# A sparse-graph layer and an eight-expert feed-forward layer in one kernel: the order of Pool's work round the last routing, and the gate's logits in one product with the turn

## The reference

```python
h  = item_feat @ W_item.T + b_item                    # 10000 x 128
x1 = x + relu(adj @ h + layernorm(x) @ W_user.T + b_user)

t      = layernorm(x1)
logits = t @ gate_w + gate_b                          # 8 experts
idx    = argmax(softmax(logits)); prb = its probability
pos    = place of the token among those of its expert, in token order
kept   = pos < 1563                                   # capacity
y      = relu(t @ w1[idx] + b1[idx]) @ w2[idx] + b2[idx]
out    = x1 + y * prb * kept                          # a token beyond capacity keeps x1
```

## Time and profile before

| | |
|---|---|
| three runs | 1380.58, 1382.54, 1383.38 us; median 1382.54 |
| the profiled execution | 1382.88 us, of which the span of its instructions is 1381.1 us |
| busy share of the span | PE 97%, DVE 85%, ACT 68%, Pool 42% |
| granted TensorE clock, mean | 0.984 |
| HBM | 428.11 MB read, 23.87 MB written, 327 GB/s over the span |

### The profile page before, as it was taken

The page is one execution under the profiler, slowest core; times in us unless marked ns, Lnnn a source line. Parts: engine busy times, 40 slices in busy tenths (PEclk is TensorE's granted clock), DMA queues, the critical chain, the costliest instruction groups (busy, mean ns, idle before and its releaser), DMA issues. The chain is left out here.

```text
span 1381.1 us, 19857 instructions
## 1 busy us (share of the span) xinstructions
PE 1339.5 (97%) x6152; PEld 1097.9 (79%) x6152; DVE 1169.4 (85%) x1781; ACT 945.8 (68%) x906; POOL 576.0 (42%) x335
## 2 busy tenths in 40 slices
PE   7999999999999999999999999999999999899993
PEld 6888888888888888888888888888888877677772
DVE  6999989899898898988989989889898894577774
ACT  5777767767667677676776767767767664677871
POOL 0001154262450633605426145162360563588887
PEclk9999999999999999999999999999999999899997
DMA  8999999999999999999999999999999985233220
GB/s 327 359 379 405 412 397 373 372 370 379 367 367 377 359 379 369 366 384 360 375 375 366 380 364 372 372 363 372 378 363 376 366 302 162 80 100 100 71 49 3
DMA packets 99950, 441.56 MB, mean 320 GB/s; under 512 B 29635, under 2 KB 37867, under 8 KB 99905
## 3 DMA queue, kind: packets, MB, share of 16 engines
q1 hardware_dynamic: 69017, 418.17, 80.3%
q0 software_dynamic: 24928, 12.59, 3.8%
q10 hardware_dynamic: 5960, 10.24, 2.3%
HBM read 428.11 MB, written 23.87 MB: 327 GB/s over the span
## 5 line engine op out<-in xcount | busy, mean ns | idle before, releaser
L694 DVE TENSOR_TENSOR a_lo<-raw,a_hi 128x2000 fp32r<-128x2000 f32 (+1 forms) x400 | 867.7, 2189 | 101.4 <-ACT a_hi L501 96.7
L501 ACT CAST a_hi<-raw 128x2000 fp32r<-128x2000 f32 (+1 forms) x400 | 724.8, 1826 | 287.1 <-PE bank L1109 189.5
L1107 PE MATMUL bank<-a_hi,h_hi 128*128 128x500 f32 x1560 | 622.7, 399 | 0.6 <-ACT a_hi L501 0.6
L1109 PE MATMUL bank<-a_hi,h_lo 128*128 128x500 f32 x1560 | 607.5, 389 | 0.0
L1118 PE MATMUL bank<-a_lo,h_hi 128*128 128x500 f32 x1560 | 419.0, 389 | 0.0
L1107 PEld LDWEIGHTS bank<-a_hi,h_hi 128*128 128x128 f32 x1560 | 294.3, 189 | 63.2 <-issue 5.7
L1109 PEld LDWEIGHTS bank<-a_hi,h_lo 128*128 128x128 f32 x1560 | 294.9, 189 | 60.5 <-issue 4.4
L1118 PEld LDWEIGHTS bank<-a_lo,h_hi 128*128 128x128 f32 x1560 | 293.9, 188 | 59.6
L1003 POOL TENSOR_TENSOR late<-ve,neghalf 125x4 f32<-125x4 f32 x20 | 55.3, 2763 | 597.5 <-DVE ve L711 597.5
L1011 POOL DMA_INDIRECT records<-late,slot x80 | 170.3, 2129 | 22.8 <-issue 22.8
L1075 POOL DMA_INDIRECT out<-raw x104 | 144.4, 1388 | 43.9 <-issue 33.6
(11 more groups left out here) (128 smaller groups left out, 848.0 us busy)
## 6 DMA issues: line engine op xcount, KB each, us to landing
raw<-adj_m SPq DMA_DIRECT2D x380, 1000.0 KB, 6.5
raw<-adj_m SPq DMA_DIRECT2D x20, 500.0 KB
xT<-x_t ACTq DMA_DIRECT2D x20, 250.0 KB, 4.2
late<-items_t SPq DMA_DIRECT2D x19, 256.0 KB, 4.5
raw<-records SPq DMA_DIRECT2D x24, 191.8 KB
xb<-x ACTq DMA_DIRECT2D x20, 224.0 KB
raw<-w SPq DMA_DIRECT2D x8, 258.5 KB
raw<-w SPq DMA_DIRECT2D x8, 256.0 KB
```

Of the source, the lines that this page charges most:

```text
L501: last = nc.scalar.copy(a_hi[:, g % HI_RING, 0:m], raw[:, g % RAW, 0:m])
L694: last = v.tensor_tensor(a_lo[:, g % RAW, 0:m], raw[:, g % RAW, 0:m], a_hi[:, g % HI_RING, 0:m].bitcast(F32), ALU.subtract)
L1107: nc.tensor.matmul(acc[q][:, 0:BLOCK], h_hi[:, k * HID:(k + 1) * HID], a, start=(k == 0), stop=False)
L1109: last = nc.tensor.matmul(acc[q][:, 0:BLOCK], h_lo[:, k * HID:(k + 1) * HID], a, start=False, stop=False)
```

## The change

Six things change.

1. `logits` and `turn_x1` become one product: the constants' table puts `gate_w` right behind the identity, so four matmuls by 136 columns give the turned x1 and its logits. They go to two PSUM banks, two tiles each; ACT copies them with two instructions in place of one, and `choose` on DVE scales the logits with two in place of one.
2. In block 19 this product for block 18 stands at g = 3, where logits and turn stood at g = 2.
3. `find_order` on DVE stands at g = 8 of block 19, not 14.
4. Pool issues `pass_on` of block 17 ahead of the wait for the cleared slots, and `pass_on` of block 18 ahead of `x1_scale` of block 19.
5. Slots are cleared in 120 runs of 14 for each expert (1680 slots), not 124 of 13 (1612); `clear_edges` has 112 rows, not 104.
6. Units 0 and 1 are turned back, gated and put out inside the routing of block 19, not in steps 5 and 6.

```diff
-RUN = 13
-RUNS = SLOTS_E // RUN
+RUN = 14
+RUNS = 120
+SLOTS_E = RUNS * RUN
...
+        turn_w = cst[:, COLS["ident"][0]:COLS["gate_w"][1]]
...
-                nc.scalar.copy(rec[:, q, :, 0:HID],
-                               turned[0:TP, :].rearrange("p (j d) -> p j d", j=TILES)).then_inc(x1_ready, 1)
+                for half, turned in enumerate(ps_turn_last if is_last(n) else ps_turn):
+                    last = nc.scalar.copy(rec[:, q, 2 * half:2 * half + 2, 0:HID], turned[:, :, 0:HID])
+                last.then_inc(x1_ready, 1)
...
-                dve.wait_ge(logits_done, n + 1)
+                dve.wait_ge(x1_ready, n + 1)
...
-                        if g == 14:
+                        if g == 8:
                             find_order()
...
-                if has(at, LAG_OUT, 0):
+                if at == EARLY + LAG_IN:
+                    gate_and_add(0, 0)
+                if at == EARLY + LAG_MID:
+                    gate_and_add(0, 1)
+                if has(at, LAG_OUT):
                     gate_and_add(i, k - LAG_OUT)
...
                     clear_slots()
                     clear_edges()
+                    pool.wait_ge(slots_ready, b - 1)
+                    pass_on(q)
                     pool.wait_ge(edges_cleared, 16)
                     pool.wait_ge(runs_cleared, EXPERTS * 16)
                 if not fixed or b > 1:
                     scatter(b - 2, q)
+                if not fixed or 1 < b < BLOCKS - 1:
                     pass_on(q)
...
             scatter(BLOCKS - 2, 0)
+            pass_on(0)
             x1_scale(BLOCKS - 1, 1)
-            pass_on(0)
             scatter(BLOCKS - 1, 1)
...
-            def logits(n):
+            def turn_x1(n):
                 pe.wait_ge(x1T_ready, n + 1)
                 if not isinstance(n, int) or n > 0:
+                    pe.wait_ge(x1_ready, n)
                     pe.wait_ge(shifted, n)
-                to = ps_logit_last if is_last(n) else ps_logit
+                turned = ps_turn_last if is_last(n) else ps_turn
                 for j in range(TILES):
-                    last = nc.tensor.matmul(to[:, j, :], gnn[:, j * TP:(j + 1) * TP], const("gate_w"),
+                    last = nc.tensor.matmul(turned[j // 2][:, j % 2, :], gnn[:, j * TP:(j + 1) * TP], turn_w[:, :],
                                             start=True, stop=True)
...
-                    if g == (2 if is_last(b) else 5) and (not fixed or b > 0):
-                        logits(b - 1)
+                    if g == (3 if is_last(b) else 5) and (not fixed or b > 0):
                         turn_x1(b - 1)
```

More of the change, by code:

```diff
@@ L47 @@
 UNIT = max(UNIT_TILES) * SLOT_P
-SLOTS_E = UNIT_AT[-1]
-assert SLOTS_E >= CAP and UNIT <= 512
+RUN = 14
+RUNS = 120
+SLOTS_E = RUNS * RUN
+assert SLOTS_E >= UNIT_AT[-1] >= CAP and UNIT <= 512
 SLOTS = EXPERTS * SLOTS_E
 UNITS = EXPERTS * UNITS_E
-RUN = 13
-RUNS = SLOTS_E // RUN
 EDGE = EXPERTS * RUN
-assert SLOTS_E % RUN == 0 and max(RUNS, EDGE) <= TP
+assert max(RUNS, EDGE) <= TP
 BODY = 2 * UNITS_E
@@ L74 @@
 _at = 0
-for _name, _n in (("ident", 128), ("tri", TP), ("rev", TILES * EXPERTS), ("tok", 2 * TILES),
-                  ("w_user", HID), ("gate_w", EXPERTS), ("gate_b", TILES * EXPERTS),
+for _name, _n in (("ident", HID), ("gate_w", EXPERTS), ("tri", TP), ("rev", TILES * EXPERTS), ("tok", 2 * TILES),
+                  ("w_user", HID), ("gate_b", TILES * EXPERTS),
                   ("run_at", 1), ("run_no", EXPERTS), ("edge_of", EXPERTS),
@@ L202, in build @@
         acc = bank[0:2]
-        ps_gnn, ps_x, _, ps_h0, ps_h1 = bank[2:7]
-        ps_logit, ps_logit_last = (t[0:TP, 2 * EXPERTS:(2 + TILES) * EXPERTS].rearrange("p (j e) -> p j e", j=TILES)
-                                   for t in (bank[4], bank[7]))
+        _, ps_x, _, ps_h0, ps_h1 = bank[2:7]
+        TURN = HID + EXPERTS
+        ps_turn, ps_turn_last = ([t[0:TP, a:a + 2 * TURN].rearrange("p (j c) -> p j c", j=2) for t, a in pair]
+                                 for pair in (((bank[2], 0), (bank[4], 0)),
+                                              ((bank[6], 0), (bank[7], 2 * EXPERTS))))
         ps_count = bank[7][0:TP, 0:EXPERTS]
@@ L657, in _ @@
             v = nc.vector
-            chain = Chain(dve, dve_chain, 22)
+            chain = Chain(dve, dve_chain, 23)
             x_chain = Chain(dve, x_chain_done, 2)
@@ L746, in choose @@
                 chain.round(n)
-                dve.wait_ge(logits_done, n + 1)
+                dve.wait_ge(x1_ready, n + 1)
                 dve.wait_ge(rstd_ready, n + 1)
-                raw_logit = ps_logit_last if is_last(n) else ps_logit
-                chain.link(v.tensor_tensor(lg[:, :, :], raw_logit, rec[:, q, :, C_RSTD:C_RSTD + 1].broadcast_to(
-                    [TP, TILES, EXPERTS]), ALU.mult))
+                for half, turned in enumerate(ps_turn_last if is_last(n) else ps_turn):
+                    pair = slice(2 * half, 2 * half + 2)
+                    chain.link(v.tensor_tensor(lg[:, pair, :], turned[:, :, HID:TURN],
+                                               rec[:, q, pair, C_RSTD:C_RSTD + 1].broadcast_to([TP, 2, EXPERTS]),
+                                               ALU.mult))
                 chain.link(v.tensor_tensor(lg[:, :, :], lg[:, :, :], gate_b, ALU.add))
@@ L1269, in _ @@
             turn_slots(0, 2)
+            turn_y(0, 0)
             second(0, 1, range(2, FC))
@@ L1276, in step @@
                     mid(i, k - LAG_MID)
-                if has(at, LAG_OUT, 0):
+                if at == EARLY + LAG_MID:
+                    turn_y(0, 1)
+                if has(at, LAG_OUT):
                     turn_y(i, k - LAG_OUT)
```

12 lines of the change are left out of this document (removed).

## The result

| | before | changed | changed, second comparison |
|---|---|---|---|
| median, us | 1382.96 | 1368.19 | 1370.27 (before: 1382.91) |
| runs | 4 | 4 (1366.81 to 1370.40) | 6 (1367.78 to 1371.33) |
| ratio, 95% interval | | 0.9898 (0.9879 to 0.9917) | 0.9908 (0.9890 to 0.9925) |
| profiled execution: time, span | 1382.88, 1381.1 | 1370.40, 1368.5 | span 1368.0 |

The changed kernel is faster, by 14.8 us in the first comparison and 12.6 in the second; the forecast was 13. The profiled execution, against whose time the sum was made, became 12.5 us shorter. What follows reads the changed kernel's trace against the rows of before.

What follows compares the result with a forecast made beforehand. PE bounds the blocks and units, and a chain through Pool's clearing DMAs the stretch between. Terms -5.5 + 0.2 - 8.4 + 0.6 = -13.1 us from 1382.88 give 1369.8, forecast 1370, range 1365 to 1378.

Steps and rivals of the forecast that it cites:

- The product: Logits and turn on PE: the joint product saves 0.31 us a block in 18 blocks, -5.5 us.
- The slower joint product: Rival: weight loads not hidden, the joint product takes 1.70 us and costs 8.8 us, total 1387 to 1391; chance 0.04.
- ACT's and DVE's additional instructions: About 0.2 us each, costing nothing beside PE in the blocks; DVE's stands on the chain behind block 19, +0.2 us.
- Block 19: g = 2 to 9: PE's lead is lost in a new wait of 4 to 5 us and slow clock; worth 0.
- The first weights: Order known some 18 us earlier: SP's loads start at 1146.7, about 5.7 us earlier, removing PE's 3.3 us wait for tokens.
- The clears: Landing of Pool's slot-clearing DMAs moves from 1158.93 to 1150.5, -8.4 us.
- both causes act at once: Less adjacency ahead of the clears and more evenly loaded DMA engines together: landing at 1150.5.
- the even end of 1148.5: Landing of the clears at about 1148.5 if all DMA engines were evenly loaded.
- x1_scale follows the landing one to one: Pool's twelve DMAs stay in between, so `x1_scale` of block 19 gains what the landing gains, 8.6 us at most.
- Units 0 and 1: Turned and gated inside block 19's routing: +0.6 us, between -1 and +2, with PE waiting up to 2 us.
- the clears land where they did: Rival: the landing doesn't improve, the tail gains between -1 and 4, total 1374 to 1378; chance 0.27.
- HBM bounds the blocks: Rival: HBM loads bound the blocks, the shorter product gives nothing, only the tail is left, 1375.5; chance 0.08.

Runs made afterwards that it cites:

- e1: The kernel before with only the joint product of logits and turn (point 1), still at g = 2 in block 19: 1375.01 us, ratio 0.9944.
- e7: The changed kernel with `find_order` at g = 11 of block 19 instead of g = 8: 1370.22 us, ratio 0.9925.
- e2: The changed kernel with the old clearing geometry, 124 runs of 13 slots and edges of 104 rows: 1375.27 us, ratio 0.9951.
- e9: The changed kernel with 116 clearing runs of 14 slots instead of 120, edges unchanged: 1376.53 us, ratio 0.9952.
- e5: The kernel before with only the joint product and 120 clearing runs of 14 slots, all else in the old order: 1371.70 us, ratio 0.9936.
- e11: The changed kernel run again, unaltered: 1370.27 us, ratio to the kernel before 0.9908.
- e6: The changed kernel with point 4 undone, Pool's `pass_on` of blocks 17 and 18 in their old places: 1369.05 us, ratio 0.9914.
- e3: The changed kernel with point 6 undone, units 0 and 1 turned and put out behind the routing: 1366.52 us, ratio 0.9887.
- e4: The changed kernel with `x1_scale` of block 19 ahead of Pool's `pass_on` of block 18: 1365.74 us, ratio 0.9881.
- e8: The changed kernel with the edits of e3 and e4 together: 1363.63 us, ratio to the kernel before 0.9878.
- e12: e8 run again, on the same chip as e11: 1363.78 us, ratio to the kernel before 0.9868.
- e10: e8 with `find_order` back at g = 14 of block 19: 1366.38 us, ratio to the kernel before 0.9884.

## Why the prediction was right

The mechanisms of the sum stood, and its total, but two of its terms were mis-sized, in opposite directions.

- **The product, forecast -5.5: measured -7.9** in the changed kernel's trace, 6.8 to 8.3 in all (e1: -8.2 for the whole kernel). The step that failed is the interpolation from the 372-column records. The eight records take 0.84/8 = 0.105 us each, which is what the transposes' took with 128 columns and about what the logits' took with 8 (0.099): in these rows the columns of a record, from 8 to 136, hardly matter. So the joint product costs what the eight logits' records had cost, and the transposes' 0.43 us is nearly all saved. The prediction had this case as its bound of 0.4 us a block and took the interpolated 0.31. The slower joint product, the rival that ended on the other side, is excluded.
- **ACT's and DVE's additional instructions: nothing in the blocks**, as said. The 0.2 us behind block 19 weren't measured by themselves.
- **Block 19, forecast 0: right.** The new wait is 3.45 us, forecast 4 to 5, ended by `pick`. PE is ready for the first tokens 7.8 us earlier, the blocks' part. e7 adds why its size hardly matters here: what PE gains in block 19 it gives back at the next count.
- **The first weights.** Forecast at 1146.7 - 5.5 = 1141.2, measured 1139.38, of which 2.4 us is the product's other size. PE's wait for the tokens is gone, as said. But the early order isn't enough for it: e2 and e9 know the order as early, and load the first weights at 1143.23 and 1142.17, after which PE waits 1.48 and 1.42 us. The forecast had no part of the geometry in this term.
- **The clears, forecast -8.4: measured -4.4.** The step that failed is "both causes act at once". The closed gap in the adjacency's loads gave nothing by itself: e2 has it, and its clears land at 1151.53, where before's less the 7.9 of the blocks would be at 1151.03. The 120 rows, and so, by the inference above, the even load of the engines, gave it (4.9 us in e2, 4.1 in e9; in the old order 2.5, e5 against e1), and less than the even end of 1148.5 that was reckoned: with the 7.9 us of the blocks added back the landing was at 1154.5, where the sum had 1150.5. The prediction also had the even load alone, 3.4 us and a landing at 1155.5, and should have taken that.
- **x1_scale follows the landing one to one: right** in before and in every run that kept `x1_scale` behind the twelve DMAs (18.6 to 19.3 us). Forecast at 1163.5, measured 1165.25.
- **Units 0 and 1, forecast +0.6 (-1 to +2): measured +1.8 us**, and 3.6 where the clock falls. The waits for the low parts were named, 2 us at most; the low clock behind them wasn't priced.
- **The sum**: -7.9 and -4.4 are -12.3, and the count of block 19 is 12.2 us earlier. Behind it, where point 6 costs, the profiled execution lost nothing against before. Before had its own slow clock there (0.50 from 1180 to 1190), and e1, with 0.56 from 1170 to 1180, takes 199.85 us behind its count, as before does; that the two make up for each other isn't shown further. Two errors of 2.4 and 4.0 us with opposite signs and two small ones made 13.1 where 12.5 was measured. That the total came out so near is luck: the forecast was nearer than its steps.
- **The rival "the clears land where they did"** is out; "HBM bounds the blocks" is out by e1: the product alone brought 8.2 us at the end, and PE had no gap in the blocks at a DMA share of 0.99.

## What to carry to other kernels

- Where a wait is for the landing of many small indirect DMAs, try their number of rows before their bytes or their order: here 120 rows in place of 116 or 124 were worth 4 to 5 us of landing in the new order and 2.5 in the old, while the reordering around them was worth nothing without it.
- Reordering one queue pays only if the instruction that others wait for is the one moved forward. Pool's new order exchanged four DMAs for four and gained nothing; with `x1_scale` moved to the front of them it gained 2.4 to 4.5 us.
- Work put into a gap of one engine must fit on all engines it uses. Units 0 and 1 fitted PE's gap, and filled DVE's, which the next unit needed.

## What the runs showed that was not expected

- **The number of rows also sets the time of issue.** Pool takes 0.99 us for a clearing DMA of 120 rows (the shortest of eight), 1.26 with 116 and 1.31 with 124 (e9, e2). And Pool's own queue has fewer packets with 120 rows than with 116 or 124 (24928 in e2): its entry in the profile's third part is, for e9,

```profile
q0 software_dynamic: 24672, 12.64, 4.0%
```

  and for the changed kernel, with 32 rows more,

```profile
q0 software_dynamic: 21984, 12.87, 3.8%
```

- **PE's clock behind the count of block 19 went with its wait there, with one exception.** Over 1170 to 1175 and 1175 to 1180 it was 0.73 and 0.66 in the changed kernel with a wait of 3.09 us, 0.76 and 0.66 in its repetition e11 with 2.96, 0.80 and 0.66 in e6 with 2.54. It was 1.00 throughout in e3 with a wait of 1.28, and in e4, e8 and e12 with none. But in e10, with no wait at the count either, it was 0.68 and 0.98. What sets it, the runs don't tell.
- **What a narrow product in plain 32-bit costs here is its records, not its columns, up to 136 of them.** 8, 128 and 136 columns took 0.099, 0.1075 and 0.105 us a record (372 took 0.3125). A transpose is one record in the trace, a product two: four transposes took 0.43 us and four products 0.79 (8 columns) and 0.84 us (136 columns). So beside the logits the turn was nearly free; beside the turn the logits would not be.
